# State scan of a graph network: where the decay scaling and the read-out product run

## The reference, cut to what matters

```
A = -jnp.exp(A_log)                                  # 256 channels x 16 states
dA = jnp.exp(dt[:, :, None] * A)
dBx = (dt * xc)[:, :, None] * Bm[:, None, :]
def step(h, t):
    dA_t, dBx_t, C_t = t
    h = dA_t * h + dBx_t
    return (h, h @ C_t)                              # read out: sum over the 16 states
_, y = lax.scan(step, zeros, (dA, dBx, Cm))
y = y + xc * D_param
y = y * jax.nn.silu(z)
```

## Time and profile before

| | |
|---|---|
| median of 3 runs | 10947.05 us (10939.25 to 10949.77) |
| profiled execution: its own time | 10930.7 us |
| profiled execution: its span | 10929.0 us, 1.7 us less than its time |
| busy share of the span | PE 67%, DVE 53%, POOL 36%, ACT 17% |
| instructions | 104364 |

### The profile page before, as it was taken

How to read it: one execution, slowest core, us unless ns; L and a number is a source line. 1 busy time by engine, 2 the same in 40 slices (tenths; PEclk the granted TensorE clock), 3 DMA queues, 4 the chain that set the end, 5 groups by cost and what they waited for, 6 DMA issues and landing times. The chain is left out here.

```text
span 10929.0 us, 104364 instructions
## 1 busy us (share of the span) xinstructions
PE 7270.2 (67%) x27182; PEld 4193.2 (38%) x27182; DVE 5774.2 (53%) x14785; ACT 1863.1 (17%) x4826; POOL 3941.3 (36%) x3776
## 2 busy tenths in 40 slices
PE   6976777697587586398657738743337736756846
PEld 5973333343454332266333323322113324323434
DVE  5554442222898578310167757754539938763221
ACT  0000012221264010021101101110122200112211
POOL 1665721001274374200217717610017733740021
PEclk9997678898798555699876656566669966668978
DMA  1002310100474332133123323300000013320012
GB/s 63 2 6 87 105 37 8 36 35 32 124 204 136 96 105 72 46 127 112 29 75 109 103 75 116 97 2 20 6 26 1 1 58 100 105 63 8 7 54 78
DMA packets 444260, 701.23 MB, mean 64 GB/s; under 512 B 187464, under 2 KB 289330, under 8 KB 441641
## 3 DMA queue, kind: packets, MB, share of 16 engines
q0 software_dynamic: 179840, 422.48, 14.3%
q1 hardware_dynamic: 248619, 259.00, 7.7%
q10 hardware_dynamic: 15224, 13.07, 0.4%
HBM read 620.15 MB, written 73.79 MB: 63 GB/s over the span
## 5 line engine op out<-in xcount | busy, mean ns | idle before, releaser
L2261 POOL DMA_INDIRECT R<-table,edges x2496 | 2395.1, 960 | 1540.9 <-PEq L2333 782.4
L2331 PE MATMUL PS<-R,hot 128*125 128x256 f32 (+4 forms) x4160 | 2128.5, 623 | 557.7 <-DVE hot L2287 238.7
L2331 PEld LDWEIGHTS PS<-R,hot 128*125 128x125 f32 x4160 | 917.6, 275 | 1766.6 <-DVE hot L2287 1561.7
L2307 DVE TENSOR_TENSOR acc<-acc,PS 125x256 f32 (+4 forms) x2080 | 883.3, 425 | 711.6 <-PE PS L2331 525.4
L2294 DVE TENSOR_TENSOR R<-R,TW 128x256 f32<-128x256 f32 x2080 | 872.2, 419 | 90.1 <-DMA R<-table,edges 85.5
L2287 DVE TENSOR_TENSOR hot<-iota,edges 128x125 f32<-128x125 f32 x2496 | 707.3, 284 | 41.3 <-PEq L2333 41.3
L2073 PE MATMUL PS<-S,hotT 125*128 125x100 bf16 (+1 forms) x6240 | 381.6, 216 | 513.5 <-DVE hotT L2171 500.8
L2270 ACT ACTIVATE R<-TW 128x4 f32<-128x4 f32 (+3 forms) x2080 | 411.4, 201 | 1686.8 <-PE PS L2331 1682.0
L110 POOL TENSOR_TENSOR xs<-xT 128x448 f32<-128x448 f32 x56 | 63.2, 1134 | 1347.0 <-SPq L104 1347.0
L2073 PEld LDWEIGHTS PS<-S,hotT 125*128 125x128 bf16 x6240 | 307.7, 110 | 589.0 <-DVE hotT L2171 500.5
L2328 PE MATMUL PS<-R,hot 128*125 128x258 f32 x1664 | 462.1, 400 | 85.6 <-issue 55.0
(11 more groups left out here) (672 smaller groups left out, 11086.8 us busy)
## 6 DMA issues: line engine op xcount, KB each, us to landing
rowb<-slo_row SPq DMA_DIRECT2D x260, 250.0 KB
R<-table,edges POOLq DMA_INDIRECT x2496, 2.8
W<-in_L_ffn_W1p SPq DMA_DIRECT2D x24, 1024.0 KB
W<-in_L_ffn_W2p SPq DMA_DIRECT2D x24, 1024.0 KB
W<-in_L_ffn_w SPq DMA_DIRECT2D x18, 1024.0 KB
g<-gate_rows SPq DMA_DIRECT2D x9, 1568.0 KB
hib<-hi_mask SPq DMA_DIRECT2D x260, 50.0 KB
table<-B SPq DMA_DIRECT2D x15, 625.0 KB
```

Of the source, the lines that this page charges most:

```text
L2261: pool.indirect_dma_start(R[g % RING][:, f, 0:W], None, table[:, :], bass.IndirectOffsetOnAxis(ap=G.edges[:, g * EB + f, 0:1], axis=0)).th ...
L2307: v.tensor_tensor(to, to, G.PS[0:P, k, 0:WH], ALU.add).then_inc(put, 1)
L2331: mm = pe.matmul(G.PS[0:P, k, 0:WH], hot[u][:, f, :], R[u][:, f, :], **ends)
```

## The change

The product `dt * A` moves into ScalarE's exponential, as its scale for each partition, and the lower bound of -1000 goes. ScalarE also copies the spread row of C from PSUM to a buffer `C` in SBUF, between its exponentials and `keep`. The product `hc = h * C` moves from VectorE to GpSimd and reads the copied row. `spread(m)` waits for `dB` and `C` of step `m - 2` instead of for `hc`.

```diff
-        ex, dA = [[s.sb(f"{x}{j}", [128, CW]) for j in range(2)] for x in ("ex", "dA")]
+        dA, C = [[s.sb(f"{x}{j}", [128, CW]) for j in range(2)] for x in ("dA", "C")]
...
             @block.gpsimd
             def _(pool):
-                pool.wait_ge(a_done, 2)
-                for i in range(NCH):
-                    for t in range(S):
-                        for k in range(KD):
-                            n = i * UN + t * KD + k
-                            if n >= KD:
-                                pool.wait_ge(dA_done, n - KD + 1)
-                            pool.tensor_scalar(ex[k][:, :], dt[:, k, ts(i, CW)], A[:, k, t:t + 1], -1e3, ALU.mult, ALU.max).then_inc(ex_done, 1)
+                for m in range(NCH * S):
+                    pool.wait_ge(C_done, m + 1)
+                    pool.wait_ge(h_done, (m + 1) * KD)
+                    if m >= 2:
+                        pool.wait_ge(summed, m - 1)
+                    pool.tensor_tensor(hc[m % 2][:, :, :], h[m % 2][:, :, :], C[m % 2][:, :].unsqueeze(1).to_broadcast([128, KD, CW]),
+                                       ALU.mult).then_inc(hc_done, 1)
...
                 for m in range(NCH * S):
+                    i, t = divmod(m, S)
                     for k in range(KD):
                         n = m * KD + k
-                        act.wait_ge(ex_done, n + 1)
+                        if n == 0:
+                            act.wait_ge(a_done, 2)
                         if n >= KD:
                             act.wait_ge(h_done, n - KD + 1)
-                        act.activation(dA[k][:, :], ex[k][:, :], ACT.Exp).then_inc(dA_done, 1)
+                        act.activation(dA[k][:, :], dt[:, k, ts(i, CW)], ACT.Exp, scale=A[:, k, t:t + 1]).then_inc(dA_done, 1)
+                    act.wait_ge(spread, m + 1)
+                    if m >= 2:
+                        act.wait_ge(hc_done, m - 1)
+                    act.activation(C[m % 2][:, :], PS[:, 2 * (m % 2) + 1, 0:CW], ACT.Copy).then_inc(C_done, 1)
                     if m:
                         keep(m - 1)
...
                     if m >= 2:
-                        pe.wait_ge(hc_done, m - 1)
+                        pe.wait_ge(dB_done, m - 1)
+                        pe.wait_ge(C_done, m - 1)
...
-                def read_out(m):
-                    v.wait_ge(h_done, (m + 1) * KD)
-                    if m >= 2:
-                        v.wait_ge(summed, m - 1)
-                    v.tensor_tensor(hc[m % 2][:, :, :], h[m % 2][:, :, :],
-                                    PS[:, 2 * (m % 2) + 1:2 * (m % 2) + 2, 0:CW].to_broadcast([128, KD, CW]), ALU.mult).then_inc(hc_done, 1)
...
                     if m + 1 < NCH * S:
                         drive(m + 1)
-                    read_out(m)
```

More of the change, by code:

```diff
@@ L2842, in state_scan @@
         u = s.sb("u", [128, KD, CW])
-        ex, dA = [[s.sb(f"{x}{j}", [128, CW]) for j in range(2)] for x in ("ex", "dA")]
+        dA, C = [[s.sb(f"{x}{j}", [128, CW]) for j in range(2)] for x in ("dA", "C")]
         dB, h, hc = [[s.sb(f"{x}{j}", [128, KD, CW]) for j in range(2)] for x in ("dB", "h", "hc")]
-        loaded, a_done, cleared, ex_done, dA_done, u_done, dB_done, h_done, last_done, hc_done, spread, summed, y_steps, out_done = [
-            s.sem(x) for x in ("loaded", "a", "cleared", "ex", "dA", "u", "dB", "h", "last", "hc", "spread", "summed",
+        loaded, a_done, cleared, C_done, dA_done, u_done, dB_done, h_done, last_done, hc_done, spread, summed, y_steps, out_done = [
+            s.sem(x) for x in ("loaded", "a", "cleared", "C", "dA", "u", "dB", "h", "last", "hc", "spread", "summed",
                                "y", "out")]
```

## The result

| | before | after |
|---|---|---|
| median | 10942.43 us (20 runs, 10932.48 to 10952.0) | 10927.93 us (20 runs, 10923.56 to 10935.32) |
| ratio after / before | | 0.9986, 95% interval 0.998 to 0.9993 |
| profiled execution, own time | 10930.7 us | 10933.7 us |
| first scan to last scan | 515.4 us | 493.4 us |
| the stage, from its first instruction to its last | 527.6 us | 506.6 us |

The forecast was 10928 us, with "within 0.2%" as the likeliest class. The changed kernel is faster by 14.5 us between the medians, 0.13% (the ratio of the runs gives 0.14%); the interval says 8 to 22 us. The stage itself is 21.0 us shorter in the one profiled execution of each (8209.25 to 8736.84 before, 8225.88 to 8732.47 after). The profiled execution after is longer as a whole because its untouched parts took 24 us more.

What follows compares the result with a forecast made beforehand. VectorE was taken to set the pace, with scans and GpSimd's SBUF reads taking turns. First to last scan -20.2 us and the end + 1.0 gave -19.2 from 10947.05, so 10928 us; range 10890 to 10972.

Steps and rivals of the forecast that it cites:

- within 0.2%: Whole kernel: no change beyond about 22 us, what a measurement can tell; chance 0.45.
- Who excludes whom: VectorE's scans and GpSimd instructions reading SBUF don't read at the same time; dB, with an input in PSUM, runs freely.
- Product's duration: GpSimd's new two-input product of 896 columns takes 2.07 us, priced from its two-input sum of 448 columns.
- How long it holds: GpSimd's product keeps the scans out until 1.88 us after its start, 0.19 before its end.
- Rival 1: Product holds scans to its end, or takes 2.26 us: step 4.35 us, 10949 us, no change; chance 0.20.
- The steady step: Signal 0.09, scans held out 1.88, undisturbed scan pair 2.19: 4.16 us a step against 4.18, or 4.35 in the first chunk.
- Boundaries: Where one chunk gives way to the next: extra cost 5.4 us each, six times 32.4.
- All three terms: At each chunk boundary: u delays the product 0.95 us, finish costs 1.35, TensorE's wait behind finish costs 3.1.
- the stall: TensorE's add_up waits for finish, so dB of step 3 starts 6.06 us after finish ended; cost 3.1 us.
- The end: At the stage's end the last product takes 2.07 instead of 1.08 us on the path: + 1.0 us.
- Sum: Whole kernel: -20.2 us from first to last scan and + 1.0 after make -19.2 us, 10928 us against the median.
- the expected 110 us: Naive reading that the forecast rejected: moving VectorE's product saves 1.00 us in each of 112 steps, about 110 us.

Runs made afterwards that it cites:

- e1: Changed kernel with ScalarE writing the decay dA to two free PSUM banks instead of SBUF; ratio to the kernel before 0.9903.
- e6: Changed kernel with GpSimd's read-out product replaced by a zero fill that reads nothing; 11809.6 us where the kernel before takes 11919.7.
- e9: Changed kernel with factor C left out, GpSimd's instruction reading h alone, 896 columns; 11816.4 us where the kernel before takes 11926.3.
- e8: Kernel before with ScalarE writing the decay to PSUM instead of SBUF; one execution, 10916.9 us.
- e2: Kernel before with the decay scaling moved to ScalarE alone, product kept on VectorE, GpSimd idle in the stage; ratio 0.998.

## Why the prediction was right, point by point

- **Who excludes whom.** Right, and shown from three sides: e1 takes one SBUF input from the scan, e6 both inputs from GpSimd, e9 one; each alone brings the step to 3.2 to 3.6 us.
- **Product's duration.** 2.07 us forecast, 2.08 measured. The 2.24 us from which the change would have been slower was not reached.
- **How long it holds.** 1.88 us forecast from one row of another stage, about 1.9 measured. The form "until 0.19 us before its end" fits the two-input form alone: one input of 896 columns let the scans go within the 1.12 us from GpSimd's start to theirs, of 3.20 (e9). The rule of the Trainium skill's page "SBUF — State Buffer", section "SBUF: two separate sides", that the second waits until the first instruction has finished, is right about the partners and too strict about the time; e9 decides it. Rival 1, which rested on it, falls.
- **The steady step.** 4.16 forecast, 4.20 measured, so above the 4.18 of before. The term that was off is the signal from the scan to GpSimd: I took 0.09 us from ScalarE's wait, GpSimd starts 0.13 us after (second scan to 8367.15, product at 8367.28 below). With 0.13 the sum is 0.13 + 1.88 + 2.19 = 4.20 us. Over 111 steps the error is 5 us.

```profile
8366.03 1.12 DVE L2952 TENSOR_TENSOR_SCAN h<-dA,last,dB 128x448 f32<-128x448 f32 x1
8367.07 1.06 DVE L2925 TENSOR_TENSOR u<-dt,xc 128x896 f32<-128x896 f32 x1
```

```profile
8367.28 2.79 POOL L2861 TENSOR_TENSOR hc<-h,C 128x896 f32<-128x896 f32 x1 [2.12 <-DVE h L2952]
```

- **Boundaries.** Forecast 5.4 us each, six times 32.4. Measured: 492.4 us between the end of the first pair and that of the last, less 111 x 4.205, are 25.6 us, of which 0.6 are two odd steps of 4.48; so a boundary costs 4.15 us. All three terms were too large. `u` delays the product by 0.71 us (2.79 against 2.08), not 0.95, because the product comes 0.21 us behind the start of `u` and is let in 0.14 us before `u`, of 1.06 us, ends. (In the earlier trace rows GpSimd's product starts 0.20 us ahead of `u` and not behind it: it first waited for the second scan, which ended at 8434.86, and `u` then kept it out for its own length too.) `finish` costs 1.18, not 1.35. The largest error is the stall, 2.26 us on average and not 3.1. I took over the 6.06 us from the end of `finish` to `dB` of step 3 from one boundary of the kernel before; in the changed kernel they are 4.91 to 5.41 us. TensorE's adding behind `finish` takes 3.32 us as before, but the four matmuls that spread B and C after it take less, here before and after:

```profile
8453.04 2.76 PE L2900 MATMUL PS<-X,ident 128*128 128x448 f32 x4
```

```profile
8382.82 1.90 PE L2906 MATMUL PS<-X,ident 128*128 128x448 f32 x4
```

  The granted clock was 0.50 under the adding in both, and under the spreading 0.57 before and 0.87 after. Why it rose earlier, no run shows. Behind the stall the starts of two pairs are 3.21 us apart, but that step isn't short: the second pair waits within its own duration, and from end to end it takes 4.20 us.
- **The end.** Forecast + 1.0, measured + 2.0: behind the last product the four matmuls took 2.70 us instead of 1.77. And the first scan comes 1.0 us earlier in the stage, because nobody waits for GpSimd's first product; I did not count that.

```profile
8725.20 2.07 POOL L2861 TENSOR_TENSOR hc<-h,C 128x896 f32<-128x896 f32 x1 [2.12 <-issue]
...
8727.33 2.70 PE L2898 MATMUL PS<-hc,ident 128*128 128x448 f32 x4 [2.42 <-POOL hc L2861]
```

- **Sum.** -22.0 from first scan to last, -1.0 ahead, +2.0 behind: -21.0 us in the stage against -19.2 forecast. That the median came out at 10927.9 and the forecast at 10928 is partly luck, twice over. In the stage errors of +5 us in the steps and -7 us at the boundaries nearly cancel. And the median moved by 14.5 us, not 19.2, but the base, a median of 3 runs, was 4.6 us above that of 20 (10947.05 against 10942.43), which makes up for it. Whether the 6 us between the stage's 21.0 and the runs' 14.5 are anything but the scatter of the untouched parts stays open; the interval (8 to 22 us) holds both.
- **Where the 22 us came from.** Not from the steady step, which lost 0.03 us (4.178 to 4.205, 3 us in all). The six boundaries cost 46.1 us before, reckoned in the same way, and 24.9 after: 21 us, of which the faster spreading behind `finish` gave 4.5. The first chunk and its start gave 4 us. The forecast had put 5 us of its 20 into the steps and the rest at the boundaries and the start, without a term for the spreading.
- **Where the expected 110 us went.** The step lost 1.00 us of VectorE's product and got 1.0 us of waiting in its place, inside the scan's duration. e1 gives it back.

## What to carry to other kernels

Before work moves from VectorE to GpSimd, look at which of VectorE's remaining instructions read two tensors from SBUF: here they and GpSimd's reading took turns, so a product moved between two such instructions is not hidden but put in their row. Look for such a wait in durations (a form whose maximum is far over its median), not in idle time. Where one of the two inputs can be produced in PSUM, as here in two free banks, the turn-taking ends; that was a change of one buffer and worth over four times the change itself (94 us against 22 from first scan to last). And an order of queues that wins little while another wait stands can win three times as much once that is gone, so try them together.

## What the runs showed of the hardware that was not expected

- GpSimd's exclusion of a VectorE instruction with two SBUF inputs ends before GpSimd's instruction does, and the less that one reads the sooner: two inputs of 448 columns about 0.93 us of 1.13 (one instance), two of 896 columns about 1.9 of 2.08, one of 896 columns less than 1.12 of 3.20, none 0 of 2.34.
- GpSimd's one-input instruction with two operations is slower than its two-input product of the same size: 3.20 against 2.08 us for 896 columns.
- A scan with its decay in PSUM takes what it takes from SBUF (1.134 us median in both e1 and e8, 1.133 in e2 from SBUF with GpSimd idle), and the exponential that writes there is 0.03 us faster (0.64 us in e1 against 0.67 in the changed kernel, 0.55 in e8 against 0.58 before).
